# Adaptive-norm RNN and mixture-of-experts block: the limit on the gated half moves from before its activation to after it

## The reference

```python
h = jnp.einsum('th,ehd->etd', xn, w1) + b1[:, None, :]
a = jnp.minimum(h[..., ::2], LIMIT)            # gated half, LIMIT = 7
b = jnp.clip(h[..., 1::2], -LIMIT, LIMIT)      # linear half
s = a * jax.nn.sigmoid(ALPHA * a) * (b + 1.0)  # ALPHA = 1.702
y = jnp.einsum('eti,eih->eth', s, w2) + b2[:, None, :]
t = jnp.einsum('eth,te->th', y, gate_full)
```

## Time and profile before

| | |
|---|---|
| median of 3 runs | 128.87 us (128.7 to 128.93) |
| profiled execution, span from first to last instruction | 126.7 us |
| median less that span | 2.17 us |
| busy: PE / PEld | 109.5 us (86%) / 93.9 us (74%) |
| busy: DVE / ACT / POOL | 98.0 us (77%) / 84.0 us (66%) / 69.3 us (55%) |
| granted TensorE clock, mean | 0.994 of full speed |

### The profile page before, as it was taken

One profiled execution on the slowest core, in us unless ns is written; L12 is line 12 of the kernel. 1 busy time (PEld: TensorE's weight loads), 2 busy tenths in 40 slices (PEclk: granted clock), 3 DMA queues, 4 the chain that ended last, 5 costly groups with the idle time before them and its releaser, 6 DMA issues.

```text
span 126.7 us, 2120 instructions
## 1 busy us (share of the span) xinstructions
PE 109.5 (86%) x659; PEld 93.9 (74%) x659; DVE 98.0 (77%) x242; ACT 84.0 (66%) x182; POOL 69.3 (55%) x81
## 2 busy tenths in 40 slices
PE   3579799958999978999898899689999999999750
PEld 2568589957998877999797787567888888888330
DVE  0106669998958899959998799988786887887950
ACT  4015694939976369786684558597878878878610
POOL 5200216808996697864864597645645645645600
PEclk9999999999999999999999999999999999999997
DMA  2899800000000000000000000100000100000003
GB/s 57 182 348 354 283 0 5 0 3 0 3 0 0 0 5 0 0 0 5 0 3 0 3 0 16 31 0 3 0 0 0 47 0 0 0 0 0 0 0 83
DMA packets 6190, 4.53 MB, mean 36 GB/s; under 512 B 754, under 2 KB 6100, under 8 KB 6148
## 3 DMA queue, kind: packets, MB, share of 16 engines
q1 hardware_dynamic: 6148, 4.34, 12.0%
q0 software_dynamic: 32, 0.07, 0.2%
HBM read 3.88 MB, written 0.52 MB: 35 GB/s over the span
## 4 chain that ended last, share of the span: by engine, by line
issue 28%; POOL 28%; DVE 19%; PE 13%; ACT 4%; DMA 3%; POOLq 1%; SPq 1%; DVEq 0%; ACTq 0%
POOL act_lo L407 23%; DVE lin L733 4%; DMA x_sb<-in_x 3%; PE psR L820 2%; POOL xh L387 2%; DVE hot L605 2%; DVE actg L751 2%; DVE logits L578 2%; POOL rstd L345 2%; DVE act L764 1%; PE psB L804 1%; PE psR L812 1%; PE psB L865 1%; PE psM L827 1%; POOL hot L361 1%
## 5 line engine op out<-in xcount | busy, mean ns | idle before, releaser
L407 POOL TENSOR_TENSOR act_lo<-actg,act_hi 128x512 fp32r<-128x512 f32 x31 | 40.6, 1311 | 33.4 <-ACT act_hi L467 33.4
L467 ACT ACTIVATE act_hi<-actg 128x512 fp32r<-128x512 f32 (+1 forms) x33 | 20.3, 618 | 20.9 <-DVE actg L751 20.9
L733 DVE TENSOR_SCALAR lin<-psB,one_b1b 128x256 f32<-128x256 f32 (+1 forms) x48 | 25.9, 567 | 9.5 <-PE psB L865 9.3
L501 ACT ACTIVATE relu_a<-psA,lim_b1a 128x256 f32<-128x256 f32 (+1 forms) x48 | 25.3, 536 | 1.7 <-PE psA L865 1.7
L509 ACT ACTIVATE swish<-relu_a,limit_col 128x512 f32<-128x512 f32 x32 | 23.2, 725 | 1.0
L764 DVE SCALAR_TENSOR_TENSOR act<-lin,swish 128x512 f32<-128x512 f32 x32 | 22.3, 696 | 0.4 <-ACT swish L509 0.3
L751 DVE TENSOR_TENSOR actg<-act,psG 128x512 f32<-128x512 f32 x31 | 21.0, 677 | 0.2 <-PE psG L879 0.2
L865 PE MATMUL psA<-xn_hi,w_hi 128*128 128x256 f32 (+1 forms) x48 | 17.0, 354 | 0.0
L865 PE MATMUL psB<-xn_hi,w_hi 128*128 128x256 f32 (+1 forms) x48 | 16.6, 347 | 0.0
L865 PE MATMUL psA<-xn_lo,w_hi 128*128 128x256 f32 (+1 forms) x48 | 15.6, 325 | 0.0
L865 PE MATMUL psA<-xn_hi,w_lo 128*128 128x256 f32 (+1 forms) x48 | 15.6, 325 | 0.0
(11 more groups left out here) (114 smaller groups left out, 203.3 us busy)
## 6 DMA issues: line engine op xcount, KB each, us to landing
w_sb<-in_L_ffn_w SPq DMA_DIRECT2D x4, 512.0 KB, 5.7
w_sb<-in_L_ffn_w SPq DMA_DIRECT2D x4, 256.0 KB, 5.5
x_sb<-in_x SPq DMA_DIRECT2D x1, 448.0 KB, 4.4
out<-y_sb SPq DMA_DIRECT2D x8, 32.0 KB, 1.6
out<-y_sb SPq DMA_DIRECT2D x4, 64.0 KB, 1.7
x_sb<-in_x SPq DMA_DIRECT2D x1, 64.0 KB, 2.0
wh_sb<-in_L_cond_Wh POOLq DMA_DIRECT2D x1, 64.0 KB, 2.4
wx_sb<-in_L_cond_Wx SPq DMA_DIRECT2D x1, 64.0 KB, 2.2
```

Of the source, the lines that this page charges most:

```text
L407: nc.gpsimd.tensor_tensor(act_lo[:, u % SUM_DEPTH, 0:w], actg[:, u % 3, 0:w], act_hi[:, u % SUM_DEPTH, 0:w].bitcast(F32), ALU.subtract).th ...
L467: nc.scalar.activation(act_hi[:, u % SUM_DEPTH, o], actg[:, u % 3, o], ACT.Copy).then_inc(hi_done, 1)
L501: last = nc.scalar.activation(relu_a[:, u % 2, o], psA[u % 2][:, o], ACT.Relu, scale=-1.0, bias=lim_b1a[:, e0 + k:e0 + k + 1])
L733: last = nc.vector.tensor_scalar(lin[:, v % 2, o], psB[v % 2][:, o], one_b1b[:, e0 + k:e0 + k + 1], LIMIT + 1.0, ALU.add, ALU.min)
```

## The change

ScalarE takes the activation straight from psA with bias b1a and writes swish; there is no relu pass. The limit is applied by a min with gelu(7), held as a column that ScalarE computes once (L427, which now waits for the constants). VectorE makes lin_gated(v-1) = max(lin, -6) * gates where actg(v-1) was made, and actg(v-1) = min(swish, gelu(7)) * lin_gated where act(v) was made. lay_gates waits for lin_gated in place of actg; up(v, 0) for the activation in place of the relu. Tensors relu_a, act and lim_b1a go; lin_gated, b1a and gelu_limit come. The diff without the declarations:

```diff
@@ -424,7 +424,8 @@
         def _(acte):
 
             acte.wait_ge(ident_ready, 1)
-            nc.scalar.activation(act[:, 0, 0:1], zeros[:, 0:1], ACT.Gelu_apprx_sigmoid)
+            acte.wait_ge(consts_ready, 1)
+            nc.scalar.activation(gelu_limit[:, :], limit_col[:, :], ACT.Gelu_apprx_sigmoid).then_inc(gelu_limit_ready, 1)
 
             def tanh(t):
                 acte.wait_ge(step_mm, t + 1)
@@ -491,23 +492,16 @@
                     acte.wait_ge(m_read, psM_turn("b1"))
 
                 acte.wait_ge(a_mm, u + 1)
-                if u >= 2:
-                    acte.wait_ge(swish_done, u - 1)
+                if u >= 3:
+                    acte.wait_ge(actg_done, u - 2)
                 for k in range(r):
                     if k == 1:
                         for t in steps_at(u, 0):
                             tanh(t)
                     o = part(c, k)
-                    last = nc.scalar.activation(relu_a[:, u % 2, o], psA[u % 2][:, o], ACT.Relu, scale=-1.0,
-                                                bias=lim_b1a[:, e0 + k:e0 + k + 1])
-                last.then_inc(relu_done, 1)
-
-                acte.wait_ge(relu_done, u + 1)
-                if u >= 3:
-                    acte.wait_ge(act_done, u - 2)
-                w = width(u)
-                nc.scalar.activation(swish[:, u % 3, 0:w], relu_a[:, u % 2, 0:w], ACT.Gelu_apprx_sigmoid, scale=-1.0,
-                                     bias=limit_col[:, :]).then_inc(swish_done, 1)
+                    last = nc.scalar.activation(swish[:, u % 3, o], psA[u % 2][:, o], ACT.Gelu_apprx_sigmoid,
+                                                bias=b1a[:, e0 + k:e0 + k + 1])
+                last.then_inc(swish_done, 1)
                 for t in steps_at(u, 1):
                     tanh(t)
                 for q in at(STATS, u + 1):
@@ -684,12 +678,13 @@
             nc.vector.tensor_copy(xT[:, P:4 * P], psB[1][:, 0:3 * P]).then_inc(xT_ready, 1)
 
             dve.wait_ge(ident_ready, 1)
+            dve.wait_ge(gelu_limit_ready, 1)
             link(nc.vector.tensor_tensor(pair_id[:, :], ident[:, HI:HI + E], ident[:, LO:LO + E], ALU.add))
             nc.vector.tensor_copy(select[:, :, :], pair_id[:, :].rearrange("p (e o) -> p e o", o=1)
                                   .to_broadcast([P, E, P])).then_inc(select_ready, 1)
 
             dve.wait_ge(m_mm, psM_turn("b1"))
-            nc.vector.tensor_scalar(lim_b1a[:, :], psM[:, 0:E], -1.0, LIMIT, ALU.mult, ALU.add)
+            nc.vector.tensor_copy(b1a[:, :], psM[:, 0:E])
             nc.vector.tensor_scalar(one_b1b[:, :], psM[:, E:2 * E], 1.0, None, ALU.add).then_inc(m_read, 1)
             w1_low(0)
             stats(0)
@@ -744,25 +739,27 @@
                 if 1 <= v <= NU:
                     u = v - 1
                     dve.wait_ge(g_mm, u + 1)
-                    dve.wait_ge(act_done, u + 1)
-                    if u >= 3:
-                        dve.wait_ge(lo_done, u - 2)
-                    for o in pieces(u):
-                        nc.vector.tensor_tensor(actg[:, u % 3, o], act[:, u % 2, o], gate_bank(u)[:, o],
-                                                ALU.mult).then_inc(actg_done, 1)
+                    dve.wait_ge(lin_done, u + 1)
+                    if u >= 2:
+                        dve.wait_ge(actg_done, u - 1)
+                    w = width(u)
+                    nc.vector.scalar_tensor_tensor(lin_gated[:, u % 2, 0:w], lin[:, u % 2, 0:w], 1.0 - LIMIT,
+                                                   gate_bank(u)[:, 0:w], ALU.max, ALU.mult).then_inc(gated_done, 1)
                 for q in at(RSTD, v):
                     route_top(q)
                 for q in at(RSTD, v - 1):
                     route_hot(q)
                 for q in at(GATES, v):
                     gates_inverse(q)
-                if v < NU:
-
-                    dve.wait_ge(lin_done, v + 1)
-                    dve.wait_ge(swish_done, v + 1)
-                    w = width(v)
-                    nc.vector.scalar_tensor_tensor(act[:, v % 2, 0:w], lin[:, v % 2, 0:w], 1.0 - LIMIT,
-                                                   swish[:, v % 3, 0:w], ALU.max, ALU.mult).then_inc(act_done, 1)
+                if 1 <= v <= NU:
+                    u = v - 1
+                    dve.wait_ge(gated_done, u + 1)
+                    dve.wait_ge(swish_done, u + 1)
+                    if u >= 3:
+                        dve.wait_ge(lo_done, u - 2)
+                    for o in pieces(u):
+                        nc.vector.scalar_tensor_tensor(actg[:, u % 3, o], swish[:, u % 3, o], gelu_limit[:, 0:1],
+                                                       lin_gated[:, u % 2, o], ALU.min, ALU.mult).then_inc(actg_done, 1)
                 if v + 3 < NP:
                     w1_low(v + 3)
                 if v == 0:
@@ -874,7 +871,7 @@
                 if u == NU - 1:
                     pe.wait_ge(m_read, psM_turn(("out", NC - 2)))
                 elif u >= 1:
-                    pe.wait_ge(actg_done, u)
+                    pe.wait_ge(gated_done, u)
                 for k in range(r):
                     last = nc.tensor.matmul(gate_bank(u)[:, k * n:(k + 1) * n], select[:, e0 + k, :], gT[:, cols(c)],
                                             start=True, stop=True)
@@ -964,7 +961,7 @@
                     if v == UNIT0[c]:
                         pe.wait_ge(xn_ready, last_group(c) + 1)
                     if v >= 2:
-                        pe.wait_ge(relu_done, v - 1)
+                        pe.wait_ge(swish_done, v - 1)
                     up(v, 0, psA[v % 2], a_mm)
                     for t in steps_at(v, 0):
                         step(t)
```

More of the change, by code:

```diff
@@ L102, in adaln_rnn_moe_kernel @@
         b_col = sb("b_col", [P, 2])
-        lim_b1a = sb("lim_b1a", [P, E])
+        b1a = sb("b1a", [P, E])
+        gelu_limit = sb("gelu_limit", [P, 1])
         one_b1b = sb("one_b1b", [P, E])
@@ L135, in adaln_rnn_moe_kernel @@
         gT = sb("gT", [P, NT * P], F32R)
-        relu_a = sb("relu_a", [P, 2, W])
         swish = sb("swish", [P, 3, W])
         lin = sb("lin", [P, 2, W])
-        act = sb("act", [P, 2, W])
+        lin_gated = sb("lin_gated", [P, 2, W])
         actg = sb("actg", [P, 3, W])
@@ L193, in adaln_rnn_moe_kernel @@
         y_mm = sem("y_mm")
-        relu_done = sem("relu_done")
         swish_done = sem("swish_done")
         lin_done = sem("lin_done")
-        act_done = sem("act_done")
+        gelu_limit_ready = sem("gelu_limit_ready")
+        gated_done = sem("gated_done")
         actg_done = sem("actg_done")
```

## The result

Both kernels ran on the same chip: 140.29 us after the change (median of 4 runs, 140.18 to 140.32), 128.90 us before (4 runs, 128.7 to 129.43). The ratio is 1.087, with a 95% interval of 1.084 to 1.090. The span of the profiled execution is 138.3 us in place of 126.7, and the mean granted clock 0.955 in place of 0.994.

The account below looks back on a forecast made before the run. PE alone paced the last chunk; earlier, DVE and PE waited for each other through ACT and POOL. Terms 6.25 + 4.2 + 0.9 - 0.95 + 0.7 = 11.1 us made the 126.7 us span 137.8, plus 2.17: 140.0 us; range 133.5 to 143.5.

Parts of the forecast that it names:

- What goes: On ACT, one of two sets of activation passes goes; gain taken as 0, between 0 and 2.5 us.
- term (6): Groups before the last chunk: new DVE and POOL meetings cost 0.9 us; a gate_parts subtraction no longer held gives -0.95.
- Term (1): Router's start at v = 4, 8, 12: rstd, queued behind act_lo, comes later and delays logits; 3 x 0.75 = 2.25 us.
- Term (2): RNN step, first two of three groups: later actg plus hot delay act_hi and PE's tanh; 2 x 1.25 = 2.5 us.
- Terms (3) and (4): Last chunk's gates (gT copied behind act_hi(15)) and the tail (act_lo(30) holding PE's last matmuls): 0.75 us each.
- Term (5): Last chunk: POOL's act_lo holds actg, a 2.66 to 2.75 us loop replaces PE's 2.33; 14 steps cost 4.2 us.
- Rival (A): Last chunk and tail: actg never held by POOL, only the order costs; 135.1 or 133 us; chance 0.18.
- Term (7): Last unit, made in two pieces: the second is held by act_lo(30); 0.7 us, bounds 0 and 1.3.
- Rival (B): RNN steps: ACT held the recurrence, so less ACT work makes it faster, some 126.4 us; chance 0.05.
- (C): DVE: the scalar_tensor_tensor reading psG takes the time of two passes, 1.35 us; 150 us total; chance 0.03.
- (D): Whole kernel: the change does nothing because PE absorbs all; chance 0.04.

Follow-up runs that it names:

- e5: Kernel before with one activation pass straight from psA, limit as a number in the old act pass, lower clip left out: 128.86 us, ratio 1.0005.
- e3: Kernel before with one activation pass straight from psA, limit as a gelu(7) column in the old act pass, lower clip left out: 130.69 us, ratio 1.014.
- e7: Changed kernel with POOL's rstd moved ahead of act_lo in the same iteration: 137.63 us, ratio 1.067.
- e8: Kernel before with POOL's rstd moved ahead of act_lo in the same iteration: 126.56 us, ratio 0.982.
- e9: e7 with act_hi(u-2) run behind the activation of unit u, in units up to 12: 134.46 us, ratio 1.045.
- e10: e8 with act_hi(u-2) run behind the activation of unit u, in units up to 12: 128.89 us, ratio 1.0006.
- e1: Changed kernel with lin_gated written back into the gate bank, so actg has one SBUF tensor: median 137.77 us, ratio 1.053 from its two fastest runs.
- e4: Changed kernel with POOL's act_lo cut to 8 of 512 columns in units 16 to 30: runs of 136.99, 137.21, 137.21 and 134.48 us.
- e6: Changed kernel with dummy matmuls on PE in waits before RNN steps and in the last units: runs of 142.37, 142.47, 143.07 and 139.69 us.
- e12: Changed kernel with lin_gated in the gate bank, the limit as a number, rstd first and act_hi late: 130.37 us, ratio 1.005.

## Why the prediction was right

The time (140.29 for 140.0) held, and so did the mechanism: a later actg on chains that end on DVE and PE, and a hold by POOL that moves the bound of the last chunk. The split of the first of these into terms did not. One by one:

- *What goes* (taken as 0): right, shown by e5. The bound given to the column, "up to 0.07 us", was near its price, 62 ns; what e3 lost by it, 1.8 us, is by its rows mostly the collision of term (6) met in the other order.
- *Terms (1) to (4) and (6)*: 5.96 us for 6.2, a sum that held with parts that did not. Term (1), 2.25 us: logits' waits grew as predicted, by 3.7 - 1.4 = 2.3 us, but they are not a price of their own. With rstd moved in both kernels (e7, e8) the two are 11.1 us apart where they were 11.4, and 5.5 us where they were 5.96 at the first mark. Term (2), 2.5 us: e9 took 3.1 us back to that mark (87.82 to 84.74), with the clock at 1.0 up to there in both profiled executions; that is more than predicted, and with it the stretch is as long as in e10 (84.70), though 2.4 us longer than in e8 (82.34). So the later actg reaches DVE by the router and PE by the tanh, and mending one chain leaves most of the loss to the other: the terms overlap, and adding them was not right. The split of term (2) between the later actg and hot wasn't shown. Terms (3) and (4) weren't tried alone. The stretch also holds 3.4 us at half clock, for which nothing was set aside; from e1's executions (138.06 us with 6.8 us of it, 135.5 and 135.9 at a mean clock of 0.986) an estimate is 1.2 us.
- *Term (6)*: of the 0.9 us for new meetings, xn_hi was held for 1.37 us in the first group only; in the others (63.22 and 78.99 us) it slipped in front, as the lower bound had allowed. The shorter subtraction behind the -0.95 us came true: gate_parts took 0.19 us in all groups in place of the earlier trace rows's 1.15. What it was worth on the path wasn't tried.
- *Term (5)*, 4.2 us: 3.86 us. The period was mostly 2.64 us, each link as worked out (they add up to 2.66 to 2.71, not to the 2.75 given), and e1 and e4 show its cause. Rival (A) is out.
- *Term (7)*, 0.7 us: the one that was mis-sized. The tail is 1.78 us longer. The second piece of actg(31) was held as predicted, but the clock fell too (0.50 of full from 129.2 us on). The timeline of the tail, against the earlier trace rows:

```profile
128.62 1.90 DVE L761 SCALAR_TENSOR_TENSOR actg<-swish,gelu_limit,lin_gated 128x256 f32<-128x256 f32 x2
...
128.78 1.45 POOL L407 TENSOR_TENSOR act_lo<-actg,act_hi 128x512 fp32r<-128x512 f32 x1 [1.35 <-ACT act_hi L468]
...
130.29 0.79 PE L900 MATMUL psY<-act_lo,w_hi 128*128 128x512 f32 x1 [0.59 <-POOL act_lo L407]
...
133.19 1.12 PE L999 MATMUL psA<-ident,yT 128*128 128x128 f32 x4 [0.52 <-DVE yT L785]
```

The two pieces take 1.90 us in place of 0.75, and the product with act_lo 0.79 us in place of 0.50. With the clock at 1.00 (e6) the tail was 9.6 us, 1.1 longer than before; so an estimate is 1.1 of the 1.78 us for the hold, for which 0.7 was predicted, and 0.7 for the clock. In e1, without the hold, the tail is 8.6 us: both go with it.

- *Rival (B)* is out: act_hi waited 29.4 us for actg. *(C)* is out: lin_gated took 675 ns. *(D)* too.

The near match of the total is in part luck. Nothing was set aside for the clock, which is in it with 0.7 us in the tail and an estimated 1.2 us in the first stretch; that stretch still came out 0.2 us cheaper than its sum, so that its other terms were too large together by about what the clock took. The last chunk came out 0.3 us cheaper.

## What to carry to other kernels

Ask of every pass on DVE where its operands lie and what POOL does meanwhile, and not only how long it is: moving one operand from PSUM to SBUF turned a 0.75 us pass into one of 1.35 us and moved the bound from PE to a loop over three engines. Taking work from an engine that waits gives nothing (22 us here), while a short producer such as rstd, queued behind a long wait on its engine, is worth moving even where its own wait looks small: 1.4 us of waits in the profile gave 2.3 us, another 0.5 us having been hidden in the length of a held pass. And price a change by mending a chain in both kernels, not in one: e7 alone would have put 2.7 us down to the change, e7 and e8 together leave 0.4.

## What the runs showed of the hardware

**The granted clock fell in the middle of the kernel, not in every execution.** In the kernel after PE had waited 1.51 us for tanh until 46.66 us; over the stretch from 46.66 to 50.40 us the clock is 0.57 of full, which is mostly the lower of the two levels, 1.2 GHz. From 127 us on, where PE waits 0.5 to 0.8 us for each part, it is about that again:

```profile
46.66:50.40 3.74, 3.74 (x19) 3.74 (x20) 3.67 (x8) 0.60 (x2) 3.37 (x4) 0.57 0.00 0
```

```profile
127.00:138.30 11.30, 4.93 (x11) 2.28 (x11) 5.42 (x9) 1.85 (x4) 1.89 (x2) 0.59 0.10 23
```

But e7, where PE waited 1.90 us for tanh until 50.69 us, kept the clock at 1.0 up to its tail:

```profile
44.00:52.00 8.00, 5.57 (x46) 5.16 (x45) 7.97 (x23) 4.06 (x11) 5.49 (x6) 1.00 0.00 0
52.00:60.00 8.00, 7.67 (x63) 7.09 (x62) 5.12 (x17) 3.96 (x11) 4.64 (x5) 1.00 0.01 2
```

The dips differ between executions of one kernel: e12's runs lie 4.4 us apart in bands of their mean clock, e1's also 4.4 us, while e8, with the clock at 1.0 in its profile, keeps within 0.4 us. So these kernels, whose PE waits more, were also less repeatable. Which wait sets a dip off was not isolated: a wait before the fall is not enough, as e7 shows, and e6 filled some of them, and moved the fall.

**What a held DVE pass costs.** From the third actg of the last chunk on each ended 0.55 us behind POOL's instruction, the same as act did in the earlier trace rows; the xn_hi cast of 256 columns ended 0.15 us behind it. A pass with one operand in PSUM was not held at all (725 to 751 ns in e1). The Trainium skill ("SBUF — State Buffer", section "SBUF: two separate sides") tells of a port pair that one of the two engines holds for a whole instruction. e1 and e4 agree with it, for a scalar_tensor_tensor with two SBUF tensors against a tensor_tensor on GpSimd.
